# A four-layer program: attention loads issued in the norm before, the third attention in one pass, a copy back awaited at the end, q/k/v weights first

## The chip, the cores and the metric

The kernel runs on one core of one Trainium2 chip. TensorE multiplies matrices out of SBUF into PSUM (eight banks of 128 x 512 floats); VectorE, ScalarE and GpSimd do the elementwise work, SyncE issues the DMAs. The profile calls them PE (with PEld for weight loads), DVE, ACT, POOL and SP; a q behind the name is the engine's instruction queue. Engines meet at semaphores. The metric is the device time of one execution in microseconds; lower is better.

## The reference

All is float32, x has 4 batches of 512 tokens of 128 channels. Four layers of the same frame, each with an attention and a gating branch of its own:

```python
for layer in range(4):                    # as the kernel stages it
    xn = layernorm(x)
    x  = x + attention[layer](xn) * silu(ffn[layer](xn))
```

Layer 0: window attention (16 heads of 8, window 32) and attention over 64 pooled latents, mixed by gates; its ffn quantizes to fp4 values. Layer 1: causal attention with 16 heads of 64; a ternary ffn. Layer 2: differential causal attention, 32 query heads of 8 channels over 8 key heads, two softmaxes subtracted with a learned lambda; its ffn is a transformer of six layers (16 heads of 64, window 32, rotary positions with a scale):

```python
def attn_layer(x, Wqkv, qs, ksc, Wo):     # once per layer of the ffn
    q, k, v = jnp.split(x @ Wqkv, 3, -1)  # then by heads
    q, k = l2norm(q) * qs, l2norm(k) * ksc
    q = q * cos * scale + rotate_half(q) * sin * scale
    k = k * cos / scale + rotate_half(k) * sin / scale
    return local_attention(q, k, v) @ Wo
```

Layer 3: a gated linear recurrence over 16 states per channel, followed by a layernorm; its ffn is a transformer of two layers (8 heads of 64, window 64).

## The kernel before

The whole state lives in SBUF: `x`, its norm `xn`, the transposed norm `xnT` (128 channels x 2048 tokens), and two results `s` (attention) and `u` (ffn). `program` runs one stage after the other: `load_inputs`, and then for each layer `between` (lines 2798 and following: multiply `s` with the SiLU of `u`, add to `x`, normalize, transpose), the attention, the ffn; at the end `between` once more, with the way out to DRAM.

Each stage is a `Stage` (L41). When it ends, SyncE clears the stage's semaphores, one instruction each (L59), and all engines meet at a barrier (L60). No engine has anything to do for the next stage before that, and a stage's buffers are free behind it. So nothing of one stage overlaps anything of another.

**Loads of an attention.** Each attention has a block in which SyncE issues its weights and masks (L870 to 882: 14 loads; L1656 to 1662: 7; L2111 to 2116: 8; L2554 to 2566: 8) on the semaphore `loaded`, and in which the engines wait until all have landed. In the fourth attention GpSimd also clears a matrix, `power[:, 0]` (L2693), into whose diagonal blocks SyncE then loads the matrices `A` by 8 more DMAs; behind it GpSimd clears three more, `mV`, `mW` and `mT`. At its end the fourth attention writes its result to DRAM and reads it back in another layout:

```python
sp.dma_start(s[:, :, :], ds.rearrange("(n p) m -> p n m", p=P)).then_inc(s_back, 16)   # L2593
sp.wait_ge(s_back, 16)                                                               # L2594
```

`s` is next read in the last `between`, a whole transformer later.

**The transformers** (`transformer`, L198; `ffn2` and `ffn3` call it). SyncE issues the rotary table `base` and the mask (L363, L364), then `load(0)`: w_qkv, w_o, w_1, the norm's vectors, the scales `q_scale` and `k_scale`, w_2 and the biases (L347 to L361), all on one semaphore `w_in` whose count `w_ready(l)` stands for. `project` on TensorE (L444) waits for `w_ready`, and so does `make_tables` on VectorE (L661), which multiplies the table by the scales into `t_rot` (L666 and the following line). The path to the first result is: TensorE projects (L449), ScalarE squares (L590), VectorE reduces the squares (L672), behind its tables.

**The third attention** (`attention2`). GpSimd spreads the weights into padded forms `wq` and `wk` (each head's 8 channels take 32 columns, the rest are zeros), TensorE projects and turns the values (`va`). Then comes a loop over two halves of the batches:

- A fill block. 32 banks are filled on TensorE, 16 for Q (each 8 matmuls of 256 columns, L2177) and 16 for K (one matmul of 512 columns, L2181), over eight PSUM banks, and read out in turn by ScalarE (even ones, L2196 to 2201) and VectorE (odd ones).
- A block with 16 units, one per batch and key head (4 query heads each). A unit has 8 scores (L2275: 8 matmuls that put in the causal mask, and L2278: 2 of queries by keys), whose maxima VectorE takes (L2365); a transpose of these maxima and VectorE's `shift` that subtracts them from Q (L2372); 12 chunks of transposed scores (L2289), of which ScalarE takes the exponential (L2342); the weighing of the values (L2307), copied to `oS`, turned (L2316), and divided by VectorE. The scores run two units ahead of the chunks: units -2 and -1 of the loop are scores alone, and the last one is a drain.

The order on TensorE is written out in the list `order`. Everything but the scores goes through a ring of the four banks `B` (`claim`): a job may begin when the job four places before it was read out. `a_A` holds the scores. In the profile this stage's tiles begin with `a_`, as those of every attention do; the transformers' begin with `t_`.

## Time and profile before

| | before |
|---|---|
| three runs | 4175.67, 4182.23, 4178.7 us; median 4178.7 |
| the profiled execution | 4177.53 us, of it the span 4175.8 |
| busy: PE, PEld | 3727.0 us (89%), 2537.5 (61%) |
| busy: DVE, ACT, POOL | 2876.0 (69%), 2445.6 (59%), 2305.8 (55%) |
| mean granted clock of TensorE | 0.958 |

The stages' stretches in the span, from the time line: loading to 8.3; layer 0: norm to 20.0, attention to 300.4, ffn to 386.0; layer 1: norm to 404.8, attention to 833.6, ffn to 992.0; layer 2: norm to 1012.1, attention to 1514.5, transformer to 3558; layer 3: norm to 3578, attention to 3706, transformer to 4162; the last stage to the end.

The shares of busy time are a mean over stages of very different kinds: in the transformers TensorE, VectorE and GpSimd are all near full, in the norms none is. What a change at one place is worth is read from the instructions around that place, in the rows below. In a row of the time line stand: start, duration, engine, line, operation, output <- inputs with their shapes, the count, and in brackets how long the engine was idle before, with what released it. In a row by stretch stand: begin and end, length, the busy time and (behind an x) the instructions of PE, PEld, DVE, ACT and POOL, the mean granted clock of TensorE as a part of full speed, the DMA engines' busy share, and GB/s.

### The profile page before, as it was taken

Reading aid. Unit: us, or ns where it says so; the run is one execution under the profiler, and the core shown is the slowest. Engines: PE = TensorE matmul, PEld = TensorE weight load, DVE = VectorE, ACT = ScalarE, POOL = GpSimd, SP = SyncE. Lnnn points to the kernel's source line nnn. Section 1 sums busy time; section 2 is a strip of 40 time slices with the busy share of each in tenths; the row PEclk is TensorE's granted clock in tenths of the full one; section 3 lists DMA queues with packets and bytes.
Section 4 is the critical chain, followed back from the end, with each engine's and each line's share of the span. In section 5 each row is a group of like instructions: output and inputs, shape, how many; then the busy total and the mean of one; then the engine's idle time right before and its main releaser. Section 6 shows DMA issues by size and latency. Waiting matters only on the chain. (4 is left out here: it accounts for less than half of the span.)

```text
span 4175.8 us, 100713 instructions
## 1 busy us (share of the span) xinstructions
PE 3727.0 (89%) x40109; PEld 2537.5 (61%) x40109; DVE 2876.0 (69%) x6495; ACT 2445.6 (59%) x5007; POOL 2305.8 (55%) x2225
## 2 busy tenths in 40 slices
PE   7975999997999979999999999999999998758886
PEld 4653555543665646666666666666666666646665
DVE  3346445411665648888888888888888887548885
ACT  2222555523454547777777777777777776437775
POOL 1004000001121248888888888888888886247773
PEclk9996999998999989999999999999999999879998
DMA  0000000000000012112112112112111111120010
GB/s 20 2 8 22 1 1 1 2 27 7 2 2 2 2 56 58 41 41 67 41 41 67 41 42 66 43 41 67 41 41 41 41 41 29 33 68 22 22 24 20
DMA packets 103246, 128.49 MB, mean 31 GB/s; under 512 B 38232, under 2 KB 55680, under 8 KB 101888
## 3 DMA queue, kind: packets, MB, share of 16 engines
q1 hardware_dynamic: 102784, 122.05, 10.9%
q8 instruction: 325, 5.32, 0.5%
q14 instruction: 137, 1.12, 0.1%
HBM read 31.95 MB, written 3.54 MB: 8 GB/s over the span
## 5 line engine op out<-in xcount | busy, mean ns | idle before, releaser
L398 POOL TENSOR_TENSOR t_inv<-t_ssq,half 128x8 f32<-128x8 f32 x448 | 779.6, 1743 | 89.9 <-DVE t_ssq L674 69.7
L449 PE MATMUL t_wa<-t_w_qkv,t_resid 128*128 128x512 f32 x1344 | 695.0, 617 | 57.4 <-DMA t_b<-in_L_ffn_b 54.6
L409 POOL TENSOR_TENSOR t_ra<-t_qn,t_rot 128x512 f32<-128x512 f32 x448 | 569.7, 1272 | 84.6 <-DVE t_qn L681 76.1
L598 ACT ACTIVATE t_p<-t_p 128x384 f32<-128x384 f32 (+1 forms) x448 | 241.0, 538 | 331.4 <-DVE t_p L698 322.4
L707 DVE TENSOR_TENSOR t_ra<-t_ra,t_rb 128x512 f32<-128x512 f32 x448 | 309.5, 713 | 123.6 <-POOL t_rb L411 123.6
L478 PEld LDWEIGHTS t_T<-ident,t_p 128*96 128x96 f32 (+1 forms) x1792 | 191.7, 128 | 312.2 <-ACT t_p L598 280.2
L410 POOL TENSOR_TENSOR t_rb<-t_qn,t_rot 128x256 f32<-128x256 f32 x448 | 367.6, 821 | 0.0
L411 POOL TENSOR_TENSOR t_rb<-t_qn,t_rot 128x256 f32<-128x256 f32 x448 | 333.1, 744 | 0.0
L449 PEld LDWEIGHTS t_wa<-t_w_qkv,t_resid 128*128 128x128 f32 x1344 | 212.5, 192 | 176.5 <-issue 146.8
L672 DVE TENSOR_REDUCE t_ssq<-t_sq 128x8 f32<-128x512 f32 x448 | 304.7, 680 | 13.9 <-ACT t_sq L590 10.4
L486 PE MATMUL t_T<-ident,t_ra 128*128 128x128 f32 x1792 | 269.1, 277 | 42.5 <-ACT t_gg L637 31.9
L2358 POOL TENSOR_SCALAR_AFFINE_SELECT a_pt<-a_pt 128x512 f32<-128x512 f32 x128 | 79.7, 634 | 394.6 <-ACT a_pt L2342 394.6
L478 PE MATMUL t_T<-ident,t_p 128*96 128x128 f32 (+1 forms) x1792 | 281.2, 280 | 17.4 <-ACT t_p L598 14.2
L681 DVE TENSOR_TENSOR t_qn<-t_wa,t_inv 128x512 f32<-128x512 f32 x448 | 290.6, 683 | 4.8 <-POOL t_inv L398 4.0
L2365 DVE TENSOR_REDUCE a_nmax<-a_A 128x2 f32<-128x1024 f32 (+3 forms) x256 | 205.1, 822 | 116.5 <-PE a_A L2278 114.2
L696 DVE TENSOR_REDUCE t_nmax<-t_S 128x4 f32<-128x384 f32 (+1 forms) x448 | 254.5, 568 | 37.9 <-PE t_S L469 37.9
L590 ACT ACTIVATE t_sq<-t_wa 128x512 f32<-128x512 f32 x448 | 261.1, 583 | 27.6 <-PE t_wa L449 27.6
L698 DVE TENSOR_TENSOR t_p<-t_S,t_nmax 128x384 f32<-128x384 f32 (+1 forms) x448 | 258.1, 576 | 15.4
L608 ACT ACTIVATE t_pT<-t_T 96x512 f32<-96x512 f32 (+1 forms) x448 | 262.8, 587 | 2.9 <-PE t_T L478 2.0
L643 ACT ACTIVATE t_qT<-t_T 128x512 f32<-128x512 f32 x224 | 133.8, 597 | 221.0 <-PE t_T L486 220.8
L2342 ACT ACTIVATE a_pt<-a_B 128x512 f32<-128x512 f32 (+1 forms) x384 | 175.7, 529 | 141.7 <-PE a_B L2289 141.7
L496 PE MATMUL t_S<-t_v,t_pT 96*64 96x66 f32 (+1 forms) x6656 | 258.2, 225 | 0.0
(400 smaller groups left out, 8410.1 us busy)
## 6 DMA issues: line engine op xcount, KB each, us to landing
t_v<-t_vn SPq DMA_DIRECT2D x192, 198.0 KB, 2.6
t_v<-t_vn SPq DMA_DIRECT2D x248, 132.0 KB, 2.4
t_v<-t_vn SPq DMA_DIRECT2D x144, 66.0 KB, 1.9
t_w_qkv<-in_L_ffn_Wqkv SPq DMA_DIRECT2D x6, 1536.0 KB
t_v<-t_nothing SPq DMA_DIRECT2D x48, 66.0 KB, 1.9
t_w_o<-in_L_ffn_Wo SPq DMA_DIRECT2D x6, 512.0 KB
f_h<-t_L_ffn_h_w SPq DMA_DIRECT2D x2, 1024.0 KB, 8.0
t_w<-in_L_ffn_W SPq DMA_DIRECT2D x6, 341.0 KB
```

Of the source, the lines that this page charges most:

```text
L398: pool.tensor_tensor(inv[:, n % 2, r, :], ssq[:, n % 2, r, :], g["half"][:, 0:8], ALU.pow).then_inc(inved.sem, 1)
L409: pool.tensor_tensor(ra[:, n % 2, r], qn[:, r], spread(cos, 1, 8), ALU.mult).then_inc(cosd.sem, 1)
L410: pool.tensor_tensor(rb[:, n % 2, r, :, 0:32], qn[:, r, :, 32:64], spread(sin[:, 0:32], 1, 8), ALU.mult).then_inc(sind.sem, 1)
L411: pool.tensor_tensor(rb[:, n % 2, r, :, 32:64], qn[:, r, :, 0:32], spread(sin[:, 32:64], 1, 8), ALU.mult).then_inc(sind.sem, 1)
L449: pe.matmul(bank, resid[:, b, lo:lo + P], w_qkv[:, l % 2, at:at + 512], start=True, stop=True).then_inc(wa_up.sem, 1)
L478: m = pe.transpose(bank[0:KEYS, j * P:(j + 1) * P], p[:, r, j, :], ident[:, :])
L486: m = pe.transpose(bank[:, j * P:(j + 1) * P], ra[:, n % 2, r, 2 * j:2 * j + 2, :].rearrange("p h d -> p (h d)"), ident[:, :])
L590: act.activation(sq[:, r].rearrange("p h d -> p (h d)"), wa[:, wa_job[kind, n] % 3, :], ACT.Square).then_inc(squared.sem, 1)
L608: act.activation(pT[0:KEYS, r].rearrange("p h k -> p (h k)"), turned(f"p{r}", G)[0:KEYS], ACT.Copy).then_inc(T_in.sem, 1)
L672: v.tensor_reduce(ssq[:, n % 2, r, :], sq[:, r], X, ALU.add).then_inc(summed.sem, 1)
L681: v.tensor_tensor(qn[:, r], wa[:, wa_job[kind, n] % 3, :].rearrange("p (h d) -> p h d", h=8), spread(inv[:, n % 2, r, :], 2, HD), ALU.mult ...
L707: v.tensor_tensor(ra[:, turn % 2, r], ra[:, turn % 2, r], rb[:, turn % 2, r], ALU.add).then_inc(roped.sem, 1)
```

## The change

1. **Loads of the attentions.** A new class `Early` (a `Stage` whose end does not clear its semaphores) holds the weights' buffers and `loaded`. `fetch0` to `fetch3` return what SyncE is to issue, and `between` issues it first thing in the norm. The attention takes over the semaphores and clears them at its end. For the fourth attention the clearing of `power[:, 0]` on GpSimd and the 8 diagonal loads go along.
2. **The copy back.** `s_back` becomes a semaphore of the program. The fourth attention issues the DMA and does not wait; GpSimd waits for it in the last `between`.
3. **The transformers.** w_qkv and the two scales come first, on semaphores `qkv_in` of their own, then (in the first layer) table and mask, then the rest on `w_in`. `project` and `make_tables` wait for `qkv_ready`; the first `mix_heads` of a layer waits for `w_ready`.
4. **The third attention.** One fill block for batches 0 and 1, then one loop of 32 units. Q and K keep 16 slots (`HELD`). Batches 2 and 3 are filled into slots whose unit is over, in the middle of units 8 to 13 and 16 to 21, up to three banks a unit, behind the scores of steps 1, 4 and 7. Such a fill is a job of the ring `B`; for Q it is 16 matmuls of 128 columns, for K one of 512; even ones are read out by ScalarE, odd ones by VectorE.

```diff
+class Early(Stage):
+    def __init__(self, nc, name):
+        super().__init__(nc, name)
+        self.weights = []
+        self.loaded = self.sem("loaded")
+        self.loads = 0
+
+    def __exit__(self, *exc):
+        return self.ctx.__exit__(*exc)
...
+def fetch3(early, d):
...
+    def issue(sp):
+        sp.dma_start(A[:, :, :], d["L3_attn_A"]).then_inc(loaded, 16)
...
+        sp.wait_ge(emptied, 1)
+        for e in range(E):
+            sp.dma_start(power[16 * e:16 * e + 16, 0, :, 16 * e:16 * e + 16], d["L3_attn_A"].rearrange("(g e) a b -> e a g b", e=E)[e]).then_inc(blocks, 16)
+
+    def prepare(pool):
+        pool.memset(power[:, 0], 0.0).then_inc(emptied, 1)
...
-def between(nc, g, name, gated, out):
+def between(nc, g, name, gated, out, issue=None, prepare=None):
...
             def _(sp):
+                if issue is not None:
+                    issue(sp)
...
             def _(pool):
+                if prepare is not None:
+                    prepare(pool)
                 for b in range(BATCH + 1):
+                    if out is not None and b == 0:
+                        pool.wait_ge(g["s_back"], 16)
...
-                sp.dma_start(s[:, :, :], ds.rearrange("(n p) m -> p n m", p=P)).then_inc(s_back, 16)
-                sp.wait_ge(s_back, 16)
+                sp.dma_start(s[:, :, :], ds.rearrange("(n p) m -> p n m", p=P)).then_inc(g["s_back"], 16)
...
                         if n % SLOTS == 0:
-                            pe.wait_ge(*w_ready(l))
+                            pe.wait_ge(*qkv_ready(l))
...
                     pe.wait_ge(T_in.sem, T_in.at(copied["o", t * NG + NG - 1]))
+                    if t % TILES == 0:
+                        pe.wait_ge(*w_ready(l))
...
                 def make_tables(l):
-                    v.wait_ge(*w_ready(l))
+                    v.wait_ge(*qkv_ready(l))
...
-    HALVES = 2
-    NB = BATCH // HALVES
-    UNITS = NB * NKV
+    NB = 2
+    UNITS, HELD = BATCH * NKV, NB * NKV
...
+        FILL_AT = (1, 4, 7)
+        def fills(u, h):
+            b, n = u // NKV + 1, 3 * (u % NKV) + FILL_AT.index(h)
+            return [(b, n)] if NB <= b < BATCH and n < 16 else []
...
+                if h in FILL_AT:
+                    order += [("fill", *job) for job in fills(u, h)]
...
+                def fill(b, n):
+                    bank = claim("fill", b, n)
+                    toks = xnT[:, b * SEQ:(b + 1) * SEQ]
+                    if n < 8:
+                        for r in range(4):
+                            for j in range(GH):
+                                m = pe.matmul(bank[32 * j:32 * j + 32, r * P:(r + 1) * P].rearrange("p (u t) -> p u t", t=QT), wq[:, 4 * n + r, :],
+                                              toks.rearrange("p (u j t) -> p u j t", j=GH, t=QT)[:, :, j, :], start=True, stop=True,
+                                              tile_position=(0, 32 * j), skip_group_check=True)
+                    else:
+                        m = pe.matmul(bank, wk[:, n - 8, :, :].rearrange("p j e -> p (j e)"), toks, start=True, stop=True)
+                    m.then_inc(B_up.sem, 1)
```

On ScalarE and VectorE a fill is read out in one instruction, behind the exponentials or the maxima of the same step. Three places show how the instructions move. First SyncE, between the norm of layer 1 and the attention behind it; an ISA row is that many semaphore clears, a branch row the beginning or end of a block. Before:

```order
L2823 UNCONDITIONAL_BRANCH
L59 ISA x12
L1654 UNCONDITIONAL_BRANCH
L1656 DMA a_wv<-in_L_attn_w_v 128x1024
L1657 DMA a_wq<-in_L_attn_w_q 128x1024
L1658 DMA a_wk<-in_L_attn_w_k 128x1024
L1659 DMA a_wu<-in_L_attn_w_u 128x8x128
L1660 DMA a_bu<-in_L_attn_b_u 128x128
L1661 DMA a_place<-c_place 128x256
L1662 DMA a_mask<-c_qmask 128x256
```

The same place on SyncE in the changed kernel:

```order
L2828 UNCONDITIONAL_BRANCH
L2976 DMA w_wv<-in_L_attn_w_v 128x1024
L2977 DMA w_wq<-in_L_attn_w_q 128x1024
L2978 DMA w_wk<-in_L_attn_w_k 128x1024
L2979 DMA w_wu<-in_L_attn_w_u 128x8x128
L2980 DMA w_bu<-in_L_attn_b_u 128x128
L2981 DMA w_place<-c_place 128x256
L2982 DMA w_mask<-c_qmask 128x256
L2827 UNCONDITIONAL_BRANCH
L60 ISA x12
L1632 UNCONDITIONAL_BRANCH
L1631 UNCONDITIONAL_BRANCH
```

The seven loads stand inside the norm's block, ahead of its twelve clears, and the attention's block on SyncE holds a wait alone. Then SyncE at the beginning of layer 2's transformer. Before:

```order
L363 DMA t_base<-c_rot 128x1024
L364 DMA t_mask<-c_bmask 128x192
L347 DMA t_w_qkv<-in_L_ffn_Wqkv 128x3072
L348 DMA t_w_o<-in_L_ffn_Wo 128x8x128
L349 DMA t_w<-in_L_ffn_W 128x682
```

In the changed kernel:

```order
L352 DMA t_w_qkv<-in_L_ffn_Wqkv 128x3072
L353 DMA t_scales<-in_L_ffn_q_scale 128x64
L354 DMA t_scales<-in_L_ffn_k_scale 128x64
L356 DMA t_base<-c_rot 128x1024
L357 DMA t_mask<-c_bmask 128x192
L358 DMA t_w_o<-in_L_ffn_Wo 128x8x128
```

The projections' weights moved from third to first place, and the scales from behind the output weights to the second and third. Last TensorE in a unit of the third attention, around a score of the step that a fill follows; `a_A` are the score banks, `a_B` the ring. Before:

```order
L2275 MATMUL a_A<-a_place,a_cmask 128x128 x8
L2278 MATMUL a_A<-a_K,a_Q 128x256 x2
L2289 MATMUL a_B<-a_Q,a_K 128x256 x2
L2275 MATMUL a_A<-a_place,a_cmask 128x128 x8
L2278 MATMUL a_A<-a_K,a_Q 128x256 x2
L2316 MATMUL a_B<-ident,a_oS 128x128 x4
```

In a unit with fills of the changed kernel:

```order
L2276 MATMUL a_A<-w_place,w_cmask 128x128 x8
L2279 MATMUL a_A<-a_K,a_Q 128x256 x2
L2256 MATMUL a_B<-xnT,a_wq 32x128 x16
L2290 MATMUL a_B<-a_Q,a_K 128x256 x2
L2276 MATMUL a_A<-w_place,w_cmask 128x128 x8
L2279 MATMUL a_A<-a_K,a_Q 128x256 x2
L2317 MATMUL a_B<-ident,a_oS 128x128 x4
```

A fill of 16 matmuls has come between a score and the next chunks; the rest of the unit stands in the same order.

## Rows read from the trace of the kernel before

**Rows 1.** busy by stretch: us, busy us (x) by engine, clock, DMA, GB/s

```profile
8.30:20.00 11.70, 4.35 (x16) 2.86 (x16) 7.40 (x48) 6.87 (x14) 4.37 (x5) 1.00 0.00 0
...
386.00:404.80 18.80, 4.35 (x16) 2.87 (x16) 11.96 (x52) 7.77 (x16) 9.67 (x8) 0.50 0.00 0
...
1035.50:1065.00 29.50, 27.97 (x290) 15.95 (x292) 17.62 (x24) 18.10 (x24) 0.00 (x0) 1.00 0.00 1
...
1065.00:1084.70 19.70, 17.29 (x196) 9.86 (x198) 12.82 (x16) 0.00 (x0) 0.00 (x0) 0.68 0.01 1
...
1085.00:1237.00 152.00, 151.23 (x2200) 103.30 (x2200) 102.63 (x168) 80.98 (x172) 32.38 (x52) 0.99 0.01 2
```

**Rows 2.** time line, VectorE, the first attention's beginning

```profile
20.03 2.29 DVE L913 TENSOR_REDUCE a_xl<-xnT 128x256 f32<-128x2048 f32 x1 [3.47 <-PEq L60]
...
28.67 0.42 DVE L915 TENSOR_TENSOR a_gprod<-a_gw,a_wraw 128x256 f32<-128x256 f32 x1 [6.36 <-DMA a_masklq<-c_masklq]
```

**Rows 3.** time line, TensorE, the second attention's first matmul

```profile
414.18 3.78 PE L1687 MATMUL a_T<-a_wv,xnT 128*128 128x512 f32 x4 [11.15 <-DMA a_mask<-c_qmask]
```

**Rows 4.** time line, the third attention's beginning

```profile
1012.17 0.12 POOL L2093 MEMSET a_w<- 128x32 f32 x1 [4.62 <-POOLq L60]
...
1020.12 5.64 PE L2126 MATMUL a_A<-xnT,a_w 128*32 128x512 f32 x32 [10.24 <-DMA a_place<-c_place]
```

**Rows 5.** time line, the fourth attention's beginning

```profile
3577.97 1.80 POOL L2693 MEMSET a_power<- 128x2048 f32 x1 [4.12 <-POOLq L60]
...
3584.34 5.31 PE L2641 MATMUL a_Y<-xnT,a_wg 128*128 128x512 f32 x8 [8.14 <-DMA a_bet<-in_L_attn_beta]
```

**Rows 6.** time line of SyncE, and the DMA issues: KB, us to landing

```profile
3697.36 0.74 SPq L2593 DMA_DIRECT2D s<-a_ds  x1
...
3706.01 0.35 SPq L363 DMA_DIRECT2D t_base<-c_rot  x1
...
s<-a_ds SPq DMA_DIRECT2D x1, 0.5 KB, 6.3
```

**Rows 7.** time line, the beginnings of both transformer stages

```profile
1514.49 0.33 SPq L363 DMA_DIRECT2D t_base<-c_rot  x1
...
1527.31 5.46 PE L449 MATMUL t_wa<-t_w_qkv,t_resid 128*128 128x512 f32 x6 [16.45 <-DMA t_b<-in_L_ffn_b]
...
1528.56 0.28 DVE L666 TENSOR_TENSOR t_rot<-t_base,t_scales 128x128 f32<-128x128 f32 x1
...
1529.45 0.60 ACT L590 ACTIVATE t_sq<-t_wa 128x512 f32<-128x512 f32 x1 [11.11 <-PE t_wa L449]
...
1530.08 0.69 DVE L672 TENSOR_REDUCE t_ssq<-t_sq 128x8 f32<-128x512 f32 x1 [1.24 <-ACT t_sq L590]
...
3718.92 0.69 DVE L672 TENSOR_REDUCE t_ssq<-t_sq 128x8 f32<-128x512 f32 x1 [1.24 <-ACT t_sq L590]
```

**Rows 8.** busy time by stretch, while the first transformer's loads run

```profile
1514.50:1516.50 2.00, 0.00 (x0) 0.00 (x0) 0.06 (x1) 1.97 (x2) 2.00 (x1) 0.81 0.45 98
...
1516.50:1518.50 2.00, 0.00 (x0) 0.00 (x0) 0.00 (x0) 1.85 (x1) 2.00 (x3) 0.50 1.06 410
```

**Rows 9.** time line, VectorE's shifts in steady units

```profile
1228.10 0.68 DVE L2372 TENSOR_TENSOR a_Q<-a_B,a_Q 128x512 f32<-128x512 f32 x1
...
1239.63 0.68 DVE L2372 TENSOR_TENSOR a_Q<-a_B,a_Q 128x512 f32<-128x512 f32 x1
```

**Rows 10.** time line, fills and weighing of the third attention

```profile
1035.54 3.66 PE L2177 MATMUL a_A<-xnT,a_wq 128*32 128x256 f32 x64 [0.89 <-PEq L2090]
...
1267.71 3.66 PE L2177 MATMUL a_A<-xnT,a_wq 128*32 128x256 f32 x64 [1.39 <-PEq L2248]
...
1183.13 0.56 PEld L2307 LDWEIGHTS a_B<-a_pt,a_va 128*32 128x32 f32 x12 [0.19 <-issue]
...
1050.66 1.18 ACT L2201 ACTIVATE a_K<-a_A,a_kone 128x512 f32<-128x512 f32 x1 [0.84 <-PE a_A L2181]
```

**Rows 11.** waits, 1085 to 1237: waiter <- releaser: us, count, longest

```profile
PEld a_A L2275 <- DVE a_nmax L2365: 10.0, 25, 0.7
```

More of the change, by code:

```diff
@@ L840, in attention0 @@
         logit_up = st.sem("logit_up")
-        LOADS = 4 + 4 + 2 + 4
+        LOADS = early.loads
         with nc.Block() as block:
@@ L2912, in program @@
         }
+        g["s_back"] = ctx.enter_context(nc.semaphore("s_back"))
+        nc.sync.sem_clear(g["s_back"])
         load_inputs(nc, g, dram)
         for layer in range(4):
-            between(nc, g, f"norm{layer}", layer > 0, None)
-            ATTENTION[layer](nc, g, dram)
+            with Early(nc, f"w{layer}") as early:
+                issue, prepare = (fetch0, fetch1, fetch2, fetch3)[layer](early, dram)
+                between(nc, g, f"norm{layer}", layer > 0, None, issue, prepare)
+                ATTENTION[layer](nc, g, dram, early)
             FFN[layer](nc, g, dram)
```

673 lines of the change are left out of this document (371 added, 302 removed).

## The prediction, made before the changed kernel ran

> **What bounds the kernel now.** I read the profile in three steps. First the busy time by stretch [rows 1]: with one core there is one chain of stages, each ending at a barrier, so a stage that ends earlier moves everything behind it by the same amount. Then, at each stage that the change touches, the time line around its first instructions: what the first matmul waits for [rows 2 to 7]. Then the inside of the third attention: how long one of its units takes and what TensorE waits for there [rows 9 to 11].
>
> Three things are to be seen. The norms before the attentions take 11.7 us (the first) and 18.8 and move nothing by DMA (0 GB/s) [rows 1]; the attention behind it then starts by issuing its loads and waits for the last of them. The fourth attention ends on a DMA that nobody reads before the end of the program. And the third attention does one thing twice: 29 us in which TensorE fills Q and K, then about 20 us of scores alone, then a long stretch in which TensorE is busy 151.2 of 152.0 us, at granted clock 0.99; then it drains, and the second half repeats all of it. In the long stretch VectorE is at 102.6 and ScalarE at 81.0 us of 152 [rows 1], so both have room.
>
> **The change part by part.** The profiled execution took 4177.5 us (its span 4175.8, and 1.7 around it); the median of the runs shown is 4178.7, 1.2 above it.
>
> *Loads of the four attentions moved into the norm.* SyncE has nothing else there. The longest list, 14 issues, is issued and landed within 8.7 us (20.0 to 28.67) [rows 2], the heaviest, the second attention's, within 9.4 of the stage's begin [rows 1, 3]. So even the first norm's 11.7 us cover them whole; if that cover were gone, each stage would wait as now. What is late next:
> First attention: VectorE's reduction from 20.03 takes 2.29 us and must run anyway; behind it VectorE sat idle 6.36 us until the last load [rows 2]. TensorE and GpSimd hang on the same wait. Gain 6.3 us.
> Second: the norm ends at 404.80 [rows 1], TensorE's first matmul starts at 414.18, and nothing is done between [rows 3]. Gain 9.3 us.
> Third: the stage's first memset ends at 1012.3, and it is all that the first matmul needs beside the loads; it ran at 1020.12 [rows 4]. The other memsets are needed only behind the first matmuls. Gain 7.8 us.
> Fourth: stage begin 3577.97, first matmul 3584.34 [rows 5]. Gain 6.3 us. GpSimd's clearing of the first matrix (1.80 us) [rows 5] goes into the norm too, where GpSimd has nothing to do until ScalarE's first SiLU is ready. The three matrices that it still clears in the stage are 5.4 us by the same row, so its products of the gate come less than 6.3 us earlier; what is made of them, by way of DRAM, is read only by the first state matmuls, late in the stage, so I cost that at nothing (at most 3 us).
>
> *The fourth attention's result awaited at the end.* SyncE issues the copy back at 3697.36 (0.74 us) and the next stage begins at 3706.01 [rows 6]. It lands 6.3 us after its issue [rows 6]; then come 2.3 us of semaphore clears and barrier, which stay. The wait that goes is 6.3 - 0.74 = 5.6 us. At the end of the program GpSimd waits for a transfer that landed a whole stage before: nothing.
>
> *First projections apart.* Before, the two transformer stages wait for all loads: VectorE's first reduction of squares starts at 1530.08, 15.6 us after its stage begins, and at 3718.92, 12.9 us after [rows 6, 7]. Now the weights of q, k and v and the scales come first, then the table and the mask. In the first 2 us of such a stage the DMA engines move 98 GB/s, in the next 410 [rows 8]. For the third layer the projections' weights are 1.57 MB: 0.2 in the first 2 us, the rest in 3.3, landed at 5.3; table, mask and scales are 0.64 MB, 1.6 us, landed with their own latency near 7.2. VectorE makes its tables in 1.5 us (1527.3 to 1528.8) and reduces at 8.7. TensorE starts at 5.4, and ScalarE's square is ready 2.7 us later (1527.31 to 1530.05) [rows 7], so the tables are last. Gain 15.6 - 8.7 = 6.9 us. For the fourth the weights are half as large and land at 4.6, if I give 0.6 us for the copy back, whose landing now falls 3.3 us into the stage; tables made at 8.0. Gain 12.9 - 8.0 = 4.9 us. Bounds: nothing, if the loads share the engines evenly and all land together as now; 9 and 7, if the table lands with the first weights. The wait for the other weights moves to the first mixing of heads, far behind the 12.8 us in which all of them land today: nothing.
>
> *The third attention in one pass.* Without fills, what does the second half cost when it merely continues? Units follow each other every 11.52 us [rows 9]. The second half now takes from 1267.71 as long as the first, which took 1267.71 - 1035.54 = 232.2 us [rows 10]. Sixteen more units are 184.3 us. So 47.9 us go: one fill stretch, one stretch of scores alone at clock 0.68, one drain. Against that stand the 32 bank fills of batches 2 and 3, now inside units 8 to 13 and 16 to 21. Their price on TensorE is read from the fill stretch: 27.97 us busy for the same 32 banks of 512 columns [rows 1]. That part is not saved, only moved: 47.9 - 28.0 = 19.9 us.
> Two things modify it. TensorE waits for VectorE's maxima 10.0 us in the 152 us stretch [rows 11], 0.76 us a unit, and two of the three places of the fills (behind the second and the last score of a unit) lie where it waits. Twelve units could give back 9 us; I take 5, as VectorE has the odd fills to read out itself. Second, a Q fill is now sixteen matmuls of 128 columns instead of eight of 256. By the 27.97 us, four of 256 columns side by side come every 0.22 us; the nearest rows with 128 columns and the same 128x32 weights are in the weighing, where the last 12 weight loads, 4 of them for 256 columns and 8 for 128, take 0.56 us together [rows 10]. They go at the rate of the columns, so I add nothing. The upper bound is that a pair costs what it costs now whatever its width: 13.8 us more.
> That row also bears on a rule. The Trainium skill (TensorE: Matmul & The Clock Gate, "The mechanism") says that weight loads overlap running matmuls "only when row_grp differs". All tiles of a fill use all rows, so by this rule each load would stand in line, and narrower matmuls would cost more: rival A below, 4125 for 4106; the row of the weighing speaks against it, a long run of such fills stands in no trace yet.
> The read-outs are the same elements as before, 1.18 us for a bank [rows 10], sixteen on ScalarE and sixteen on VectorE. With three fills a unit grows by some 2.6 us on TensorE and by about 1.8 us on each of the two, which leaves both below TensorE. Queued behind a fill on ScalarE are the exponentials, on VectorE the maxima; the ring of four banks gives TensorE two chunks of scores and a tile of maxima's scores before it needs either.
> Gain 19.9 + 5 = 25 us. The stage also clears 11 semaphores fewer. The 2.3 us above hold 31 clears and a barrier, so eleven are worth 0.8 us at most: 0.5.
>
> Sum: 6.3 + 9.3 + 7.8 + 6.3 + 5.6 + 6.9 + 4.9 + 25 + 0.5 = 72.6. 4177.5 - 72.6 = 4104.9; set on the median, **4106 us**, 1.7% less.
>
> **The rivals.** A: fills cost more on TensorE, by narrow matmuls or by weight loads in line. 32 fills at 27.97 + 13.8 us, none of it in waits: the pass gains 6 us, total 4125. For it: nothing in the trace has a long row of such narrow groups of four. Against it: the weighing.
> B: the starts give half. A wait for loads may have covered another that now ends last (GpSimd's clearings, ScalarE's tables), or the transformer's loads may land together. Starts, copy back and first projections are 47.1 us; half of it leaves 4130.
> C, the one that ends slower: each fill stops TensorE for its read-out, and the clock falls. The place is the twelve units with fills; the price is 32 stops of 1.2 us (38 us), and the clock of the stretch of scores alone, 0.68 for 0.99 (a mix of its levels 1.2 and 2.4 GHz, where TensorE works between waits for VectorE) [rows 1]: twelve units of 11.52 us grow by 63, the fills by 13. Then the pass loses 94 us, where it would have won 20; with 47.6 won elsewhere the total is 4178.7 + 94 - 47.6 = 4225. It decides from the point where stops and clock cost over 68 us (20 + 47.6); below that the other gains keep the kernel ahead. Against it: behind each fill TensorE has two chunks and a score to do before it needs a read-out.
> D: the pass gives back every wait and the loads land at their upper bounds (2 + 2 us): 19.9 + 9 for the pass, and some 8 us more than forecast in all, 4098 or below.
> That the change does not do what it says would be loads queued behind something in the norm; SyncE waits there for nothing but one clearing in the last layer, so I leave it within B.
>
> **How the numbers follow.** Forecast 0.60, A 0.17, B 0.13, C 0.04, D 0.06. The forecast's own range is 4099 to 4117. To leave out no more than 2 in 10 I take in A and B and stop at 4131, and give D's edge 2 us: 4096 to 4131. A measurement of this kernel tells about 0.2%, 8 us, from no change. Only C is slower: 0.04. Within 0.2% would need C at a little over half its price: 0.01. Faster: 0.95.
>
> **What would show it.** After: no stretch of loads between a norm and its attention, and first matmuls at the beginning of each stage; two lone intervals of over 5 us gone before the transformer stages' first matmuls, with VectorE's tables the last thing before the first reduction of squares; the fourth attention's end 5 to 6 us shorter. In the third attention one fill stretch, units of 11.52 us where there is no fill, of 13.4 to 14.1 where there are three, and a stage of 502 - 7.8 - 25 - 0.5 = 469 us. Units of 15 us or more mean A or C; the granted clock tells which. A stage that starts early but whose later parts don't come earlier means B. The forecast is wrong if the stage of the third attention is above 480 us, or the others together gain under 35.

## The result: 1.4% less, 56 us where the forecast had 73

The changed kernel took 4116.7 to 4124.15 us in four runs, median 4123.6; the kernel before took 4179.2 (four runs, 4175.67 to 4182.23). The ratio is 0.9858, 95% interval [0.9845, 0.9872]. The forecast was 4106, range 4096 to 4131: inside the range and faster as forecast, but 17.6 us above the number named, and outside the forecast's own 4099 to 4117. Between profiled runs the time fell from 4177.5 to 4123.8, by 53.7. The prediction also named a sign by which it would be wrong: the third attention above 480 us, or the other gains together under 35. The third attention is at 478.3, but the others together come to 29.7 us, so by this sign the forecast failed although the total lies in its range.

The page of the changed kernel, its span and the busy time of the engines:

```profile
span 4122.1 us, 101183 instructions
...
PE 3719.1 (90%) x40355; PEld 2527.8 (61%) x40365; DVE 2877.2 (70%) x6487; ACT 2448.5 (59%) x4999; POOL 2308.0 (56%) x2225
```

TensorE is busy 7.9 us less than before (3727.0), some 1.6 of it only because this trace lacks ten matmul records in the first attention (249.81 us, where the run with the early loads alone, as long there, has all of them and 251.43); the rest of the gain is idle time that is gone. By stage, in one profiled run each, with what was forecast (stage ends read from the barriers in the time lines):

| stage | before | after | moved | forecast |
|---|---|---|---|---|
| first attention | 280.5 | 276.1 | -4.4 | -6.3 |
| second attention | 428.9 | 420.6 | -8.3 | -9.3 |
| second ffn | 158.4 | 159.1 | +0.7 | 0 |
| third attention | 502.3 | 478.3 | -24.0 | -33.3 |
| transformer of layer 2 | 2043.9 | 2038.1 | -5.8 | -6.9 |
| fourth attention | 128.0 | 118.5 | -9.5 | -11.9 |
| transformer of layer 3 | 456.9 | 454.2 | -2.7 | -4.9 |

Loading, the norms, the first ffn and the last stage moved by 0.1 us at most. Every changed place gained, and every one gained less than forecast.

The starts of the attentions are as forecast. The time line of the changed kernel at the beginnings of the attentions (start, length, engine, line), which answers to [rows 2 to 5]:

```profile
22.39 0.42 DVE L899 TENSOR_TENSOR a_gprod<-w_gw,w_wraw 128x256 f32<-128x256 f32 x1
...
400.78 3.75 PE L1658 MATMUL a_T<-w_wv,xnT 128*128 128x512 f32 x4 [1.81 <-PEq L61]
...
1000.78 6.44 PE L2088 MATMUL a_A<-xnT,w_w 128*32 128x512 f32 x32 [2.48 <-POOL w_w L2061]
...
3536.49 6.70 PE L2647 MATMUL a_Y<-xnT,w_wg 128*128 128x512 f32 x8 [1.81 <-PEq L61]
```

The gates' product starts 2.3 us into its stage (8.7 before), the second attention's matmul 0.1 (9.4), the third's 0.4 (8.0), the fourth's 0.1 (6.4). No wait took the place of the ones removed. SyncE issues all loads in the norms, and they land there.

The copy back and the stage behind it, from SyncE's queue, which answers to [rows 6]:

```profile
3651.64 0.74 SPq L2600 DMA_DIRECT2D s<-a_ds  x1
3654.98 0.37 SPq L352 DMA_DIRECT2D t_w_qkv<-in_L_ffn_wqkv  x1
```

From the issue to the next stage's first issue: 3.3 us for 8.65. So 5.3 of the 5.6 forecast are there.

The transformers' first reductions of squares, which answer to [rows 7]:

```profile
1490.33 0.68 DVE L680 TENSOR_REDUCE t_ssq<-t_sq 128x8 f32<-128x512 f32 x1
...
3664.40 0.68 DVE L680 TENSOR_REDUCE t_ssq<-t_sq 128x8 f32<-128x512 f32 x1
```

They come 11.6 and 9.5 us into their stages (which begin at 1478.7 and 3654.9), for the 8.7 and 8.0 forecast: gains of 4.0 and 3.5 us instead of 6.9 and 4.9. What the first of them waited for, TensorE's first matmul, the first of VectorE's tables and ScalarE's square:

```profile
1487.44 4.66 PE L455 MATMUL t_wa<-t_w_qkv,t_resid 128*128 128x512 f32 x6 [11.70 <-DMA t_scales<-in_L_ffn_k_scale]
1488.84 0.43 DVE L672 TENSOR_TENSOR t_rot<-t_base,t_scales 128x256 f32<-128x256 f32 x1 [9.95 <-DMA t_mask<-c_bmask]
1489.59 0.60 ACT L598 ACTIVATE t_sq<-t_wa 128x512 f32<-128x512 f32 x1 [6.96 <-PE t_wa L455]
```

The matmul waited for the second scale, which lies on the semaphore of the weights, and began 8.7 us into the stage, where the forecast had 5.4. The square was ready at 1490.19 and the reduction began at 1490.33, behind the last of the tables: the two paths end within some 0.2 us of each other.

In the third attention, VectorE's shifts show the units, as in [rows 9]. Three in a row from where the fills begin:

```profile
1152.54 0.68 DVE L2388 TENSOR_TENSOR a_Q<-a_B,a_Q 128x512 f32<-128x512 f32 x1
...
1164.85 0.68 DVE L2388 TENSOR_TENSOR a_Q<-a_B,a_Q 128x512 f32<-128x512 f32 x1
...
1178.97 0.68 DVE L2388 TENSOR_TENSOR a_Q<-a_B,a_Q 128x512 f32<-128x512 f32 x1
```

Units without fills still take 11.52 us. The first interval holds one fill (12.31), the next three (14.12); then come 13.99, 14.39, 14.30 and 14.50. The six intervals of a batch are 83.6 us for 69.1 without fills, and both batches give the same: 14.5 us for 16 fills, 0.91 us a fill, 29.0 for all 32. Busy time by stretch (us; PE, PEld, DVE, ACT, POOL busy; clock, DMA share, GB/s) in five units without fills and in six intervals with them:

```profile
1094.92:1152.54 57.62, 57.52 (x844) 39.01 (x840) 38.97 (x67) 30.66 (x65) 12.49 (x21) 1.00 0.01 2
1153.37:1236.15 82.78, 82.78 (x1280) 50.63 (x1276) 54.57 (x85) 44.90 (x86) 14.47 (x24) 1.00 0.01 2
```

TensorE was full without the fills and is full with them; its clock stays at 2.4 GHz. Rival C, the fall of the clock in these units, did not come.

### The profile page after: what moved, and what is told of

It reads as the page before. It is cut to its first block and busy times, and to the rows that moved or that the text cites. A ratio compares the mean times of both kernels' runs of the same rounds, so it can differ in the third digit from the quotient of the medians.

```text
span 4122.1 us, 101183 instructions
## 1 busy us (share of the span) xinstructions
PE 3719.1 (90%) x40355; PEld 2527.8 (61%) x40365; DVE 2877.2 (70%) x6487; ACT 2448.5 (59%) x4999; POOL 2308.0 (56%) x2225
## 5 line engine op out<-in xcount | busy, mean ns | idle before, releaser
L502 PEld LDWEIGHTS t_S<-t_v,t_pT 96*64 96x64 f32 (+1 forms) x6656 | 227.0, 137 | 35.9 <-issue 35.9
```

The source lines that it names most:

```text
L502: m = pe.matmul(S[64 * b:64 * b + 64, r, j * VD:(j + 1) * VD], pT[0:KEYS, r, j, 64 * b:64 * b + 64], windows[b][0:KEYS, 2 * j + r, :], sta ...
```

## Experiments

Three questions were open: where the pass lost 8 us to the forecast, why the transformers' first reductions came later than forecast, and why the attentions' stages lost 1 to 2 us although their first work starts as early as forecast.

### Each part alone

Four kernels, each with one part of the change and the rest as before. The loads of the attentions alone:

```diff
-    between(nc, g, f"norm{layer}", layer > 0, None)
+    between(nc, g, f"norm{layer}", layer > 0, None, issue, prepare)
```

> Only the loads of the four attentions are moved into the norm, the rest is as in the kernel before. Theory 1 (the wait goes whole, what is missing in the full change is where the granted clock falls): the first work behind each wait starts 6.1, 9.3, 7.0 and 6.3 us earlier in its stage, as in the full change; the stages end 4 to 7, 8 to 10, 6 to 8 and 4 to 7 us earlier, with differences from the full change only where the clock's half stretches lie otherwise; 27 us less in all, ratio 0.9935. Theory 2 (the start covered another wait that ends later in the stage): the stages end earlier by the same 4.4, 8.2 and 4.6 us as in the full change for the first, second and fourth attention, with equal clock stretches; 24 us less in all.

Measured: 4154.1 us (4151.9 to 4158.0), ratio 0.9928 [0.9915, 0.9942], about 30 us less; theory 1's 0.9935 lies in the interval, theory 2's 24 us (0.9943) just outside. The stages moved by -4.5, -8.3, -2.1 and -7.5. Look at the third attention: only 2.1 us less, where theory 1 had 6 to 8, although its first matmul starts 7.7 us earlier in the stage. TensorE's busy time tells why. The whole stage before, and with the early loads alone:

```profile
1012.10:1514.40 502.30, 472.65 (x6120) 304.91 (x6120) 294.22 (x484) 246.52 (x482) 87.44 (x141) 0.95 0.01 3
```

```profile
1000.20:1500.40 500.20, 478.30 (x6120) 309.38 (x6120) 294.57 (x484) 246.88 (x482) 87.38 (x141) 0.95 0.01 2
```

The length less TensorE's busy time is 29.7 us before and 21.9 now: 7.8 us of idle time are gone, as forecast. But the same 6120 matmul records were busy 5.7 us longer. By the stages' lengths alone theory 2 could claim the first and the second attention, which gave just what they gave in the full change; they also had the same mean clocks as there (0.94 and 0.99), so these two decide nothing. In the third it is the idle time that decides: it fell by what the early start takes away, which is theory 1, and the 5.7 us came back in matmuls that took longer, not in another wait.

The third attention in one pass alone:

```diff
-        for half in range(HALVES):
+        for u in range(-2, UNITS + 1):
```

> Only the third attention in one pass, the rest as before. Theory 1 (the weight loader's waits for the maxima lie under running matmuls, so a fill costs its whole time on TensorE, 0.91 us a bank): units with three fills last 14.0 to 14.5 us, 32 fills cost 29 us, the stage is 47.9 - 29.0 + 0.6 = 19.5 us shorter, give or take 3 for one half stretch of the clock more or less; ratio 0.9953. Theory 2 (the forecast: five us of waits come back, and the full change lost them to its other clock): 25.5 us, ratio 0.9939, units with fills of 13.4 to 13.8 us.

Measured: 4162.3 us (4156.3 to 4167.9), ratio 0.9947 [0.9933, 0.9960]. In the profiled run the stage takes 486.0 us, 16.3 less than before, and its units with fills have the same lengths as in the full change, to 0.02 us. The stage of the full change is 7.7 us shorter still (478.3), with the same busy time of TensorE (465.18 us): that is the early start.

```profile
1010.10:1496.10 486.00, 465.14 (x6376) 293.99 (x6376) 293.13 (x476) 245.07 (x474) 87.43 (x141) 0.96 0.01 3
```

So theory 1 has the units right; the stage's gain is 3.2 below its 19.5, just past the 3 that it allowed. On the whole time both theories lie in the interval.

The transformers' load order alone:

```diff
-                            pe.wait_ge(*w_ready(l))
+                            pe.wait_ge(*qkv_ready(l))
```

> Only the transformers' load order and their two semaphores, the rest as before. Theory 1 (the small broadcast loads behind the heavy one land one after another, 0.7 to 1.0 us each, then table and mask): first reductions of squares 4.0 and 3.5 us earlier in their stages, 7.5 us in all, less up to 3 lost or won by the clock; ratio 0.9982. Theory 2 (the forecast: the rate of the DMA engines alone sets the landing): 6.9 and 4.9, 11.8 us in all, ratio 0.9972.

Measured: 4172.0 us (4167.8 to 4177.1), ratio 0.9969 [0.9956, 0.9981]. The first reductions come 11.8 and 9.8 us into their stages, 3.9 and 3.2 us earlier than before, as theory 1 has it; the transformers are 6.3 and 2.8 us shorter. By the whole time theory 2's 0.9972 lies in the interval and theory 1's 0.9982 just above it, unless its 3 us for the clock are added; the reductions, seen in one profile, decide for theory 1.

The copy back alone:

```diff
-                sp.wait_ge(s_back, 16)
```

> Only the wait for the copy back is gone from the fourth attention, the rest as before; table and mask of the transformer behind it are issued while the copy back is under way. Theory 1: the fourth attention ends 5.6 us earlier, and the transformer's first reduction is at 12.9 us in its stage plus at most 0.6 for the shared engines; 5 us less in all, ratio 0.9988. Theory 2 (the copy back of rows of 0.5 KB slows the loads behind it by its own length): the transformer's first reduction comes 2 to 3 us later in its stage, 3 us less in all, ratio 0.9993.

Measured: 4179.9 us (4174.1 to 4185.1), ratio 0.9992 [0.9984, 1.0001]: on the whole time not to be told from nothing. In the profiled run the fourth attention is 5.2 us shorter, and the transformer's first reduction stands at 12.9 us as before, so theory 1 holds at the place. But that transformer took 3.7 us longer than before, though its code is the same and its first reduction comes at the same place. TensorE was busy 379.5 us for 377.7, which is 1.8 of them; the other 1.9 are idle time, and no run takes them apart.

### The same code at another time

The run with the load order alone has a first and a third attention that are instruction for instruction those of before, and yet 2.6 and 6.3 us longer. Its loading stage was 0.3 us shorter, so the first attention began 0.3 us earlier. In the runs with the pass alone and with the copy back alone, the same first attention took 280.2 and 280.3 us, as before. The first attention before and in that run, then the third attention in that run (the one of before is shown above):

```profile
19.90:300.40 280.50, 248.99 (x4292) 168.49 (x4292) 93.95 (x166) 76.64 (x118) 17.41 (x23) 0.96 0.02 5
```

```profile
19.60:302.70 283.10, 252.03 (x4292) 170.44 (x4292) 94.07 (x166) 76.68 (x118) 17.40 (x23) 0.95 0.02 5
1014.80:1523.40 508.60, 479.17 (x6120) 307.68 (x6120) 294.62 (x484) 246.59 (x482) 87.41 (x141) 0.94 0.01 3
```

The other engines' busy time is the same to 0.4 us. TensorE's is 3.0 and 6.5 us longer, at a mean granted clock of 0.95 for 0.96 and 0.94 for 0.95. That is a little more of the stage spent at 1.2 instead of 2.4 GHz, and it accounts for the whole difference.

Whether the 0.3 us did it is not shown, because executions of one and the same kernel differ as much. That profile is of the longest of this kernel's six runs (4177.1 us at a mean clock of 0.958, where another took 4167.8 at 0.961). The sixteen runs of the kernel before beside it went from 4177.3 us at 0.960 to 4190.5 at 0.956, and the changed kernel's four from 4116.7 at 0.966 to 4124.15 at 0.963, with no edit between them. Nor does an equal start give an equal stage. In three of the kernels here the first attention is the changed one's and begins at 20.0 us: with the early loads alone and with the fills moved (below) it took 276.0 us with 251.4 us of busy TensorE, with other rows for the scales (below) 274.2 with 249.2. The first and the last of these:

```profile
20.00:296.00 276.00, 251.43 (x4292) 170.65 (x4292) 93.97 (x166) 76.68 (x118) 17.48 (x23) 0.94 0.01 2
```

```profile
20.00:294.20 274.20, 249.19 (x4292) 168.35 (x4292) 94.00 (x166) 76.64 (x118) 17.47 (x23) 0.96 0.01 2
```

To see whether a displacement alone does this to the changed kernel, one memset of 1.8 us was put into its loading stage:

```diff
                 pool.memset(g["half"][:, :], -0.5).then_inc(halved, 1)
+                pool.wait_ge(loaded, 3 * 16)
+                pool.memset(g["u"][:, :, :], 0.0).then_inc(halved, 1)
```

> The changed kernel with one memset of 1.8 us more in the loading stage, all else the same instructions at the same distances. Theory 1 (where the half stretches of the granted clock fall depends on when a stage starts, and decides some us of it): stages of identical code differ from the changed kernel's by up to 3 to 6 us, of either sign, each with the busy time of TensorE at the half clock; the whole by 1.8 give or take 6. Theory 2 (what a stage lost to the forecast is in its instructions): each stage within 0.5 us, the whole by 1.8 to 2.5 more.

Measured: 4123.0 us (4117.6 to 4124.2), ratio 0.9856 [0.9838, 0.9875]. The loading stage is 1.9 us longer; behind it the second attention is 3.5 us shorter, the third 3.0, its transformer 3.5, the fourth attention 2.5, and the last transformer 2.9 longer. The second attention and the drain of the third (from the last shift to the end of the scores' block), first in the changed kernel, then displaced:

```profile
400.70:821.30 420.60, 404.05 (x2752) 229.10 (x2752) 203.88 (x324) 236.63 (x705) 19.71 (x32) 0.99 0.00 1
1444.90:1464.73 19.83, 17.37 (x148) 8.33 (x149) 3.59 (x13) 8.40 (x20) 4.37 (x7) 0.91 0.00 1
```

```profile
402.80:819.90 417.10, 400.38 (x2752) 227.72 (x2752) 203.75 (x324) 235.87 (x705) 19.64 (x32) 1.00 0.00 1
1443.40:1461.70 18.30, 15.85 (x150) 8.11 (x147) 3.56 (x13) 8.35 (x20) 4.35 (x7) 1.00 0.00 1
```

In the first pair the stage is 3.5 us shorter and TensorE's busy time 3.7, in the second both 1.5. Theory 2 is out: identical instructions take more or less time by several times its 0.5 us. That the displacement is what does it, as theory 1 has it, this run does not show. Its profile is of the shortest of its four runs (4117.6 us, clock 0.966), that of the changed kernel of a longer one (4123.8 us, 0.963), and the changed kernel's own shortest run, undisplaced, took 4116.7 at 0.966. So a single profiled stage of this kernel is known to some 3 us, in one stage of 502 us to 6, where the forecast added terms of 0.5 and 5. The medians of the changed kernel and the displaced one agree to 0.6 us.

### What a fill costs, and what it could give back

The forecast let 5 us of waits come back. Two kernels test that. First, the fills at the other places of a unit:

```diff
-        FILL_AT = (1, 4, 7)
+        FILL_AT = (0, 3, 6)
```

> The changed kernel with the fills behind the first, the fourth and the seventh score of a unit instead of the second, the fifth and the eighth. Theory 1 (TensorE has no idle time in a unit, the waits that the profile shows are the weight loader's and lie under matmuls): 32 fills still cost 29 us, units with three fills 14.0 to 14.5 us, third attention within 2 us of 478. Theory 2 (fills give waits back where they stand at a wait, and the places of the change are only the wrong ones): units with fills fall by 0.3 to 0.7 us each, the stage by 4 to 8 us.

Measured: 4122.7 us (4119.8 to 4125.2), ratio 0.9860 [0.9839, 0.9882]; the stage takes 479.9 us. Units with three fills last 14.3 to 14.7 us, for example these two shifts:

```profile
1162.64 0.68 DVE L2388 TENSOR_TENSOR a_Q<-a_B,a_Q 128x512 f32<-128x512 f32 x1
...
1176.92 0.68 DVE L2388 TENSOR_TENSOR a_Q<-a_B,a_Q 128x512 f32<-128x512 f32 x1
```

The fills cost 31.6 us in all here, 2.6 more than in the change. The place matters a little, against theory 2 and in the other direction; neither place gives a wait back.

Second, no fills at all:

```diff
-            return [(b, n)] if NB <= b < BATCH and n < 16 else []
+            return []
```

> The changed kernel without the fills of batches 2 and 3 (their units work on the slots of batches 0 and 1, so half of this attention's result is of the wrong batch). Theory 1 (a fill costs its whole time, 0.91 us): the stage falls by 29.0 us to 449, all units last 11.52 us, and what the pass gains over the kernel before is then 16.4 + 29.0 = 45 of 47.9 us. Theory 2 (fills return 5 us of waits): falls by 23 us.

Measured: 4090.1 us (4087.5 to 4092.3), ratio 0.9780 [0.9762, 0.9798]. Apart from the first two and the last, all intervals from shift to shift are 11.52 us, and the stage is 450.7: 27.6 us less, nearer to theory 1's 29.0 than to 23. The stage alone is known to some 3 us; the units, which repeat to 0.02 us from run to run, are the firmer figure, and they give 29.0. Its busy time, to be held against the 465.18 us of the change's stage below it:

```profile
998.70:1449.40 450.70, 436.64 (x5832) 287.56 (x5832) 276.04 (x460) 229.11 (x458) 87.39 (x141) 0.96 0.01 2
```

```profile
1000.40:1478.70 478.30, 465.18 (x6376) 294.59 (x6376) 293.21 (x476) 245.57 (x474) 87.66 (x141) 0.97 0.01 2
```

28.5 us of busy TensorE for 27.6 us of time: no idle time was filled.

### The loads ahead of the first reduction

The scales, which the change put right behind the heavy weights, were put ahead of them:

```diff
-                    sp.dma_start(w_qkv[:, z, :], wqkv[l]).then_inc(qkv_in[z], 16)
                     sp.dma_start(scales[:, z, 0, :], ...).then_inc(qkv_in[z], 16)
                     sp.dma_start(scales[:, z, 1, :], ...).then_inc(qkv_in[z], 16)
+                    sp.dma_start(w_qkv[:, z, :], wqkv[l]).then_inc(qkv_in[z], 16)
```

> The changed kernel with the two scales issued ahead of the projections' weights. Theory 1 (each small broadcast load behind the heavy one adds 0.7 to 1.0 us before table and mask can land): scales land within 4 us of the stage's begin, table and mask 1.4 us earlier than now (9.1 and 10.05 us in the third layer), and so the first reduction: 10.2 for 11.6 us, and 8.5 for 9.5 in the fourth. Theory 2 (the bytes alone set when the mask lands): landings and reduction within 0.3 us of now. On the whole time either is within 0.1%.

Measured: 4119.7 us (4115.5 to 4124.9), ratio 0.9852 [0.9831, 0.9873]. Both theories miss. Of two loads of 32 KB issued 0.4 us apart, the first landed 2.9 us into the third layer's stage and the second 5.8; the weights landed at 9.6 (6.8 in the change), the mask at 11.1 (10.1), and the first reduction came at 12.6, a microsecond later. Theory 1 had the small loads right as the slow ones, and wrong that order helps: whatever stands behind them waits.

What is slow about them was tried by itself. Each scale load reads one row of 256 bytes 128 times. Here it reads 128 different rows of the same length:

```diff
-sp.dma_start(scales[:, z, 0, :], qs[l:l + 1].to_broadcast([P, HD])).then_inc(qkv_in[z], 16)
+sp.dma_start(scales[:, z, 0, :], dram[f"c_rot{window}"][:, 0, 0, :]).then_inc(qkv_in[z], 16)
```

> The changed kernel with the two scale loads of each transformer layer reading 128 different rows of 256 bytes (out of the rotary table, so q and k are scaled wrongly) instead of one row 128 times; order, bytes and packets are the same. Theory 1 (reading one row 128 times is what is slow, and it holds up table and mask behind it): the second scale lands within 0.8 us of the weights instead of 1.9 (at most 7.5 us into the third layer's stage for 8.6 to 8.9 now), the mask at 8.3 to 8.8 for 9.9 to 10.4, the first reduction at 10.2 to 10.7 for 11.4 to 11.9. Theory 2 (small packets are slow whatever they read, or the rate of the engines alone counts): landings and reduction as now.

Measured: one run, 4118.4 us. The issues' list (KB of each, median us from issue to landing), the change first:

```profile
t_base<-c_rot SPq DMA_DIRECT2D x2, 512.0 KB, 6.9
t_scales<-in_L_ffn_q_scale SPq DMA_DIRECT2D x8, 32.0 KB, 7.0
t_scales<-in_L_ffn_k_scale SPq DMA_DIRECT2D x8, 32.0 KB, 7.4
...
t_mask<-c_bmask SPq DMA_DIRECT2D x1, 48.0 KB, 7.9
```

```profile
t_base<-c_rot SPq DMA_DIRECT2D x2, 512.0 KB, 5.5
t_scales<-c_rot SPq DMA_DIRECT2D x16, 32.0 KB, 5.9
...
t_mask<-c_bmask SPq DMA_DIRECT2D x1, 48.0 KB, 6.5
```

Theory 1 holds within 0.1 us: the mask lands 8.85 us into the third layer's stage for 10.1, and the first reductions come at 10.45 and 8.2 us for 11.6 and 9.5. Reading one row 128 times, twice, costs what is behind it 1.2 to 1.3 us in both stages of this one execution. It also costs the weights that were issued ahead of it: they landed 5.9 us after their issue in the third layer's stage for 6.7. That the source is another tensor here was not separated from it. The stretch in which it happens, in the change:

```profile
1481.80:1483.80 2.00, 0.00 (x0) 0.00 (x0) 0.00 (x0) 0.83 (x1) 1.97 (x2) 0.50 1.02 406
1483.80:1485.80 2.00, 0.00 (x0) 0.00 (x0) 0.00 (x0) 0.00 (x0) 0.00 (x0) 0.50 0.32 119
```

The DMA engines fall from 406 to 119 GB/s and a busy share of 0.32, with loads queued. With different rows the corresponding stretch stays at 344:

```profile
1482.00:1484.00 2.00, 0.00 (x0) 0.00 (x0) 0.00 (x0) 0.00 (x0) 0.00 (x0) 0.50 0.93 344
```

### A version that goes on

If waits for loads are the dependable part of this change, three more stages can be tried: both transformers and the second ffn. Their first loads were issued in the attention ahead of each. To make room, three buffers of the third attention's last block lie over its Q and K, which are no longer read by then.

```diff
+            with Early(nc, f"n{layer}") as later:
+                later.issue = (..., fetch_f1, ...fetch_ffn(e, d, 16, 32, ...), ...fetch_ffn(e, d, 8, 64, ...))[layer](later, dram)
...
                 sp.wait_ge(loaded, 7 * 16)
+                early.later.issue(sp)
...
-        attT = st.sb("attT", [P, BATCH, SEQ])
+        attT = Q[:, 0:BATCH].rearrange("p u t r -> p u (t r)")
```

> The changed kernel with the first loads of three more stages issued in the attention before each: q/k/v weights of the first layer, scales, table and mask of both transformers, and the first weights and scales of the second ffn (three buffers of the third attention's last block lie over its Q and K to make room). Theory 1 (these loads are all that the first work waits for, next is the copy of the input in ScalarE, 3.8 us, and 2.7 us to the first square): first reductions at 6.7 us in both transformer stages for 11.6 and 9.5 now, the second ffn's first matmul at once instead of 3.3 us in; 11 us less than the changed kernel, give or take 4 for the clock; ratio to the kernel before 0.983. Theory 2 (the loads in the attention take DMA time from nothing there but GpSimd's memsets end late in the stages behind): 5 us less.

Measured: 4108.8 us (4101.9 to 4111.6), ratio to the kernel before 0.9816 [0.9801, 0.9831], below the interval of the change. The starts are as theory 1 has them; the second ffn's first matmul, and the transformer's first matmul and reduction in layer 2, whose stages begin at 818.9 and 1469.4:

```profile
819.01 11.38 PE L1948 MATMUL f_bank<-xnT,n_w 128*128 128x512 f32 x22 [2.21 <-PEq L61]
...
1473.42 2.93 PE L488 MATMUL t_wa<-n_w_qkv,t_resid 128*128 128x512 f32 x3 [6.94 <-ACT t_resid L623]
...
1476.22 0.69 DVE L713 TENSOR_REDUCE t_ssq<-t_sq 128x8 f32<-128x512 f32 x1 [4.99 <-ACT t_sq L631]
```

The first matmul now waits for ScalarE's copy of the input, the reduction for the square, 6.8 us into the stage for 11.6. The median is 14.8 us below the change's, for the 11, give or take 4, of theory 1. Not every stage gained: the second ffn is 3.6 us shorter and the transformer of layer 2 6.5, but the fourth attention, in which the loads of the last transformer are now issued, took 121.8 us for 118.5, and that transformer 454.2 before and 454.4 now, though its first reduction comes 2.7 us earlier. Whether the moved loads or the clock took this is not taken apart.

## Why the prediction was right, and where it was wrong

**Loads in the norm (29.7 forecast).** Right in mechanism and, in TensorE's idle time, in size: 7.8 us in the third attention; with early loads alone 6.9 of 6.3 in the first; and in the second 25.9 us of idle time before (428.90 less the 403.02 below) and 16.6 in the change (420.60 less 404.05), 9.3 gone, as forecast. In the fourth, with early loads alone, 5.7 of 6.3. What the stages show is less, because the matmuls that now run at once do so at the lower clock, and because of where the lower clock falls later in that execution.

```profile
404.70:833.60 428.90, 403.02 (x2752) 229.10 (x2752) 203.70 (x324) 236.10 (x705) 19.63 (x32) 0.98 0.02 6
```

The waiting before was spent at the lower clock too, where it cost nothing. The third attention's first 32 matmul records show the difference: 6.44 us for 5.64 [rows 4].

**The copy back (5.6).** Right: 5.2 to 5.3 us at the place.

**The first projections (6.9 and 4.9).** The tables were last before the first reduction, as forecast, but by 0.2 us only, and the sizes were off: 4.0 and 3.5. Two steps failed. One is "TensorE starts at 5.4", when the weights land. The change counts the two scales on the weights' semaphore, so TensorE waited for them as well, until 8.7 us, and its path ended with the tables. Had the scales landed at the forecast's own 7.2 us, with table and mask, the square would have been ready at 9.9 and the gain 5.7, not 6.9 (an estimate, with the forecast's 2.7 us from first matmul to square). The other is "table, mask and scales are 0.64 MB, 1.6 us", the rate of [rows 8] applied to loads that don't go at it. The weights themselves landed at 6.75 us for the 5.3 forecast, the second scale at 8.6 and the mask at 10.1 for 7.2. The two broadcast rows are 1.2 us of the mask's 2.9 and 0.8 of the weights' 1.4, by the run with different rows; the rest was not taken apart.

**The pass (25.0).** The profiled run gave 17.0 from the first fill to the stage's end (478.9 us before, 461.9 after), the semaphores' 0.6 among it. It adds up: 47.9 - 29.0 + 0.6 is 19.5; 1.7 are lost in the drain, at clock 0.91 for 1.00, and 0.8 from the first fill to the first shift (46.4 us for 45.6), where the scores alone ran at 0.64 for 0.72. The drain before, and the scores alone before and in the change:

```profile
1481.70:1499.85 18.15, 15.70 (x149) 7.95 (x149) 3.58 (x13) 8.40 (x20) 4.35 (x7) 1.00 0.00 1
1065.00:1081.10 16.10, 14.28 (x152) 7.57 (x154) 10.69 (x13) 0.00 (x0) 0.00 (x0) 0.72 0.01 2
```

```profile
1046.30:1063.10 16.80, 15.39 (x150) 8.65 (x151) 10.88 (x12) 0.00 (x0) 0.00 (x0) 0.64 0.00 1
```

So of the 25.0 forecast 5 were waits that did not come back, 1.0 is a fill at 0.91 us for 0.87, and 2.5 are the clock of the profiled execution. The step that failed is "twelve units could give back 9 us; I take 5". The 10.0 us of [rows 11] are the weight loader's. The list of waits of that stretch has TensorE's own line as well, and it says:

```profile
PE a_A L2275 <- DVE a_nmax L2365: 0.5, 1, 0.5
```

Half a microsecond, once. The loader waited while the matmuls in front of it ran, which [rows 1] said too: TensorE busy 151.23 of 152.00 us. At most 0.8 us could be given back in that stretch. The wait did shrink when the fills came, to 0.6 us in the six intervals with fills from 3.9 in 55 us without, and returned nothing.

Rival A, the upper bound of 13.8 us on narrow fills, did not come. The seven fills of 128 columns in the first three intervals (12.31, 14.12 and 13.99 us) added 5.9 us together, 0.84 us each, against 0.86 us for one Q bank before with 256 columns (3.45 us for four, from row to row of that stretch). What made a fill dearer than 0.87 were the K fills, one matmul of 512 columns each as before: the six in the last two intervals (14.30 and 14.50) added 0.96 us each. The 32 records of a Q fill and their weight loads:

```profile
1174.40 1.08 PE L2256 MATMUL a_B<-xnT,a_wq 128*32 128x128 f32 x32
...
1174.40 0.81 PEld L2256 LDWEIGHTS a_B<-xnT,a_wq 128*32 128x32 f32 x32 [0.76 <-ACT a_pt L2354]
```

The loads lie under the matmuls, though all of them use all rows. By the rule of the Trainium skill (TensorE: Matmul & The Clock Gate, "The mechanism"), under which loads overlap "only when row_grp differs", they would have stood in line, as the prediction read it. The same section also lets a load into the "background weight buffer" go ahead of running matmuls, so it is this one sentence of it that the measurement contradicts, for these groups of four column tiles; whether that buffer is what lets them overlap no run here shows.

**Nothing took the place of the waits.** Rival B, half of the starts, is out as a mechanism in the attentions: no later wait appeared. In the transformers the loads of scales and mask kept part of the gain. In size the rival came near, since the clock and the broadcast rows took part of what the starts gave. The forecast's own range was too narrow for it: no term of the sum, and no bound, had the granted clock falling otherwise in code that the change does not touch, which differed by up to 6.3 us in a single profiled stage. That the total lies inside the range is in part luck: the range reached up to 4131 for rivals A and B, the measured 4123.6 is closer to A's 4125 than to the forecast's 4106, and A's mechanism did not come, B's in the transformers alone. Of the sum's parts the loads and the copy back were right; the first projections and the pass were not.

What stays open is why the lower clock falls where it does. The runs show that it falls otherwise from one execution to the next of the same kernel, and by how much a stage then changes. That a displacement in the program moves it was supposed here and is not shown: of each kernel one execution alone was profiled.

## What to carry to other kernels

A wait of the weight loader is not idle time of TensorE: hold it against the matmuls' busy time in the same stretch before counting on it. Loads that a stage waits for can be taken out of its start wherever the stage ahead leaves its queue and some space free, and here this gain was there in idle time in every attention; a term of less than about 3 us in a single profiled stage can't be told from where the clock's lower level falls, and before a difference is put down to an edit, the same kernel is to be profiled a second time. A semaphore that counts a load makes every engine that waits on it wait for that load, also one that never reads it. A broadcast load of one short row is not a small load: it belongs where nobody waits behind it.

## What was not expected of the hardware

Two loads of 32 KB that read one row of 256 bytes 128 times landed 2.9 us apart when they stood first in the queue, and pulled the DMA engines from 406 to 119 GB/s for 2 us when they stood behind 1.5 MB of weights; reading different rows instead gave 1.2 us back. And an unchanged stage of 502 us was 6.3 us longer in another profiled execution, all of it in TensorE's busy time, at a mean granted clock of 0.94 for 0.95.
